# Another sequence of steps in the steady turns of a recurrent mixer

## What is computed

```python
mixed = hidden_states @ W_qkv.T
y = conv1d(mixed, conv_w)                  # causal, 4 taps, one filter per channel
q, k, v = split(silu(y))
z = hidden_states @ W_z.T
beta = sigmoid(hidden_states @ W_b.T)
g = -exp(A_log) * softplus(hidden_states @ W_a.T + dt_bias)
def step(S, (q_t, k_t, v_t, g_t, b_t)):    # a scan over the tokens
    S = S * exp(g_t)
    delta = (v_t - S.T @ k_t) * b_t
    S = S + outer(k_t, delta)
    return S, S.T @ q_t
h = o * silu(z)
h = h * rsqrt(mean(h * h) + EPS) * norm_weight
out = h @ W_out.T
```

## Time and profile before

| | us |
|---|---|
| median of 3 runs | 2748.21 (2746.57 to 2750.30) |
| the profiled execution | 2751.68 |
| its span | 2750.0 |
| busy: TensorE, VectorE, ScalarE, GpSimd | 2363.9, 1981.4, 1304.2, 839.3 |
| one steady turn, from 1104.50 to 1176.40 | 71.9 |

### The profile page before, as it was taken

The page is one execution under the profiler, slowest core; times in us unless marked ns, Lnnn a source line. Parts: engine busy times, 40 slices in busy tenths (PEclk is TensorE's granted clock), DMA queues, the critical chain, the costliest instruction groups (busy, mean ns, idle before and its releaser), DMA issues. The chain is left out here.

```text
span 2750.0 us, 53589 instructions
## 1 busy us (share of the span) xinstructions
PE 2363.9 (86%) x19286; PEld 1813.9 (66%) x19286; DVE 1981.4 (72%) x4757; ACT 1304.2 (47%) x3127; POOL 839.3 (31%) x698
## 2 busy tenths in 40 slices
PE   7999998997747998889899989878487958799998
PEld 6777776885725777777777777756374845577654
DVE  4898984333368898988888888897755436787772
ACT  0444443211256777767676777774130214455232
POOL 2111100000113333333333333334876037560110
PEclk9999998998568999999999999998778977899999
DMA  4221001001412221111122222233221862220000
GB/s 158 75 76 29 14 10 51 23 24 44 156 24 51 54 53 46 45 49 50 41 51 53 52 56 55 55 82 83 77 46 25 295 188 75 73 62 1 8 21 28
DMA packets 274614, 169.24 MB, mean 62 GB/s; under 512 B 182863, under 2 KB 250590, under 8 KB 274000
## 3 DMA queue, kind: packets, MB, share of 16 engines
q1 hardware_dynamic: 248221, 140.55, 18.0%
q0 software_dynamic: 26112, 25.03, 3.5%
HBM read 99.49 MB, written 73.45 MB: 63 GB/s over the span
## 5 line engine op out<-in xcount | busy, mean ns | idle before, releaser
L1405 POOL TENSOR_TENSOR qd<-decay,qm 114x456 f32<-114x456 f32 x128 | 162.0, 1285 | 551.8 <-DVE qm L1604 464.3
L2358 PEld LDWEIGHTS d_ps<-d_xT,resid 128*128 128x128 f32 x1024 | 198.0, 195 | 47.1 <-issue 29.7
L2358 PE MATMUL d_ps<-d_xT,resid 128*128 128x228 f32 x1024 | 216.5, 363 | 12.3 <-DMA d_xT<-normed_t 12.3
L1585 DVE TENSOR_TENSOR ue<-ue,elim_tmp 128x30 f32<-128x30 f32 (+14 forms) x480 | 210.2, 438 | 16.8
L3028 POOL DMA_INDIRECT s_eo<-rows_y,slots_all x128 | 153.2, 1197 | 147.4 <-POOLq L2795 109.4
L1583 DVE TENSOR_TENSOR elim_tmp<-ue 128x30 f32<-128x30 f32 (+14 forms) x480 | 178.6, 372 | 25.2 <-issue 9.8
L1647 DVE SCALAR_TENSOR_TENSOR y_v<-raw,taps,y_v 128x228 f32<-128x228 f32 x384 | 163.4, 498 | 45.0 <-ACT y_v L2025 45.0
L1987 ACT ACTIVATE decay<-d_ps,gates 114x114 f32<-114x114 f32 x512 | 137.9, 362 | 83.7 <-DVE nt L1617 48.6
L1647 DVE SCALAR_TENSOR_TENSOR y_qk<-raw,taps,y_qk 128x228 f32<-128x228 f32 x384 | 146.5, 455 | 23.3 <-ACT y_qk L2025 23.3
L1998 ACT ACTIVATE gl<-upto,gates 114x114 f32<-114x114 f32 x512 | 156.1, 392 | 0.5 <-PE d_ps L2346 0.2
L2334 PE MATMUL d_ps<-y_qk 64*114 64x228 f32 x512 | 73.8, 411 | 95.6 <-DVE nt L1617 57.0
(11 more groups left out here) (370 smaller groups left out, 5698.9 us busy)
## 6 DMA issues: line engine op xcount, KB each, us to landing
rows_x<-zero_row SPq DMA_DIRECT2D x4, 2048.0 KB
ue<-blocks_n SPq DMA_DIRECT2D x16, 512.0 KB, 5.1
blocks_u<-ue SPq DMA_DIRECT2D x16, 512.0 KB, 3.0
blocks_v<-on SPq DMA_DIRECT2D x16, 512.0 KB, 3.1
e_x<-rows_x SPq DMA_DIRECT2D x32, 256.0 KB, 4.5
e_gu<-L_ffn_w_gate_up SPq DMA_DIRECT2D x32, 256.0 KB, 4.6
rows_y<-e_y SPq DMA_DIRECT2D x32, 256.0 KB, 3.8
blocks_n<-nt SPq DMA_DIRECT2D x96, 64.0 KB
```

The costliest lines, as they stand in the source:

```text
L1405: pool.tensor_tensor(qd[p.par][s][:, hs(u), :].rearrange("p (a o b) t -> p a o b t", o=2, b=2)[:, :, o], e[o][:, :, :].rearrange("p (a b) ...
L1585: step = dve.tensor_tensor(ue[:, 0:j, j + 1:], ue[:, 0:j, j + 1:], part, ALU.subtract)
L2358: last = pe.matmul(ps[:, f % 2, (t % 2) * W:(t % 2 + 1) * W], w_qkv[:, k, t * 128:(t + 1) * 128], xT[:, k, :], start=(k == 0), stop=(k == ...
```

## The change

Nothing is added or removed: on GpSimd, VectorE, ScalarE and TensorE the same steps stand in another sequence. On VectorE the steps of the elimination lie closer together, gate_mean 1, gate_silu 0, query_mask 2 and weights 4 and 5 come after `turn_inverse`, and the convolution comes after weights 7. On TensorE the four `value` steps stand ahead of the four `join` steps, products 3 stands behind output_turn 1, and the row steps are regrouped. On GpSimd, query_decay 4 stands between gate_power 1 and gate_scale 1. On ScalarE the reads are regrouped to match. The diff, with its indent shortened by 16 columns:

```diff
@@ -1453,24 +1453,27 @@

 def iteration(p, a=True, proj=True, z=True, d=True):
     r, done, nxt = p.shift(-1), p.shift(-2), p.shift(1)
+    if z:
+        clear_x(r, 0)
     if a:
         query_decay(p, 0)
         query_decay(p, 1)
     if d:
         gate_power(done, 0)
         gate_scale(done, 0)
-    if z:
-        clear_x(r, 0)
     if a:
         query_decay(p, 2)
+    if z:
+        clear_x(r, 1)
+    if a:
         query_decay(p, 3)
     if d:
         gate_power(done, 1)
-        gate_scale(done, 1)
-    if z:
-        clear_x(r, 1)
     if a:
         query_decay(p, 4)
+    if d:
+        gate_scale(done, 1)
+    if a:
         query_decay(p, 5)
         query_decay(p, 6)
         query_decay(p, 7)
@@ -1663,57 +1666,52 @@
     r, done, nxt = p.shift(-1), p.shift(-2), p.shift(1)
     if z:
         eliminate(r, 1, 9)
-    if a:
-        query_mask(p, 0)
-    if z:
         eliminate(r, 9, 10)
-    if a:
-        weights(p, 0)
     if d:
         gate_mean(done, 0)
     if z:
         eliminate(r, 10, 14)
     if a:
+        query_mask(p, 0)
+        weights(p, 0)
         weights(p, 1)
-    if d:
-        gate_mean(done, 1)
     if z:
         eliminate(r, 14, 23)
     if a:
+        weights(p, 2)
+        weights(p, 3)
         query_mask(p, 1)
     if z:
         eliminate(r, 23, 24)
-        gate_silu(r, 0)
-    if a:
-        weights(p, 2)
-        weights(p, 3)
     if d:
         residual(done, 0)
     if z:
         eliminate(r, 24, 29)
-    if a:
-        weights(p, 4)
-        query_mask(p, 2)
-        weights(p, 5)
-    if z:
         eliminate(r, 29, 31)
         turn_inverse(r)
+    if d:
+        gate_mean(done, 1)
+    if z:
+        gate_silu(r, 0)
         gate_silu(r, 1)
     if a:
+        query_mask(p, 2)
+        weights(p, 4)
+        weights(p, 5)
         query_mask(p, 3)
-    if proj:
-        conv(nxt, 0, 1)
-        conv(nxt, 0, 2)
-        conv(nxt, 0, 3)
-    if d:
-        residual(done, 1)
-    if a:
         weights(p, 6)
         weights(p, 7)
     if z:
         gate_silu(r, 2)
+    if proj:
+        conv(nxt, 0, 1)
+    if d:
+        residual(done, 1)
+    if z:
         gate_silu(r, 3)
     if proj:
+        conv(nxt, 0, 2)
+        conv(nxt, 0, 3)
         conv(nxt, 1, 1)
         conv(nxt, 1, 2)
         conv(nxt, 1, 3)
@@ -1723,15 +1721,13 @@
         conv(nxt, 3, 1)
         conv(nxt, 3, 2)
         conv(nxt, 3, 3)
+        silu(nxt, 0)
     if z:
         gated(r, 0)
     if proj:
-        silu(nxt, 0)
+        silu(nxt, 1)
     if z:
         gated(r, 1)
-    if proj:
-        silu(nxt, 1)
-    if z:
         gated(r, 2)
         gated(r, 3)
     ch.end()
@@ -2080,97 +2076,98 @@

 def iteration(p, a=True, proj=True, z=True, d=True):
     r, done, nxt = p.shift(-1), p.shift(-2), p.shift(1)
+    if a:
+        decay_exp(p, 0)
     if d:
         gate_squares(done, 0)
-    if a:
-        decay_exp(p, 0)
-        decay_terms(p, 2)
-        decay_exp(p, 1)
-        decay_terms(p, 3)
+        gate_squares(done, 1)
     if proj:
         raw_read(nxt, 0)
         raw_read(nxt, 1)
+    if a:
+        decay_terms(p, 2)
+        decay_terms(p, 3)
+        decay_terms(p, 4)
+        decay_exp(p, 1)
+    if proj:
         raw_read(nxt, 2)
-    if d:
-        gate_squares(done, 1)
-    if proj:
         raw_read(nxt, 3)
-        raw_read(nxt, 4)
     if a:
         decay_exp(p, 2)
     if proj:
+        raw_read(nxt, 4)
         raw_read(nxt, 5)
+    if a:
+        decay_exp(p, 3)
+    if proj:
         raw_read(nxt, 6)
-    if a:
-        decay_terms(p, 4)
-        decay_exp(p, 3)
     if d:
         oT_read(done, 0)
+    if a:
+        decay_terms(p, 5)
+        decay_terms(p, 6)
     if z:
         gate_tanh(r, 0)
     if proj:
         raw_read(nxt, 7)
     if a:
-        decay_terms(p, 5)
         decay_exp(p, 4)
-        decay_terms(p, 6)
-        decay_terms(p, 7)
     if z:
         gate_tanh(r, 1)
     if a:
+        decay_terms(p, 7)
         decay_exp(p, 5)
-    if proj:
-        decay_terms(nxt, 0)
-        first_tap(nxt, 0)
+        decay_exp(p, 6)
     if z:
         gate_tanh(r, 2)
     if d:
         oT_read(done, 1)
+    if a:
+        decay_exp(p, 7)
+    if proj:
+        first_tap(nxt, 0)
+        decay_terms(nxt, 0)
+    if z:
+        gate_tanh(r, 3)
     if proj:
         first_tap(nxt, 1)
-    if a:
-        decay_exp(p, 6)
-        decay_exp(p, 7)
+        first_tap(nxt, 2)
     if z:
-        gate_tanh(r, 3)
         join_read(r, 0)
-        join_read(r, 1)
         rhs_read(r, 0, 0)
         rhs_read(r, 0, 1)
+        join_read(r, 1)
         join_read(r, 2)
-        rhs_read(r, 0, 2)
-        rhs_read(r, 0, 3)
+        join_read(r, 3)
         inverse_read(r, 0)
         inverse_read(r, 1)
-    if proj:
-        first_tap(nxt, 2)
-    if z:
         inverse_read(r, 2)
-        join_read(r, 3)
-        x_read(r, 0, 0)
-        x_read(r, 0, 1)
-        x_read(r, 0, 2)
-        inverse_read(r, 3)
+        rhs_read(r, 0, 2)
     if proj:
         first_tap(nxt, 3)
     if z:
+        x_read(r, 0, 0)
+        x_read(r, 0, 1)
+        inverse_read(r, 3)
+        rhs_read(r, 0, 3)
+        rhs_read(r, 1, 0)
+        x_read(r, 0, 2)
+    if proj:
+        decay_terms(nxt, 1)
+    if z:
         x_read(r, 0, 3)
-        rhs_read(r, 1, 0)
         rhs_read(r, 1, 1)
         rhs_read(r, 1, 2)
         x_read(r, 1, 0)
+        rhs_read(r, 1, 3)
     if proj:
         tanh(nxt, 0)
     if z:
         x_read(r, 1, 1)
-        rhs_read(r, 1, 3)
         x_read(r, 1, 2)
+        x_read(r, 1, 3)
     if proj:
         tanh(nxt, 1)
-    if z:
-        x_read(r, 1, 3)
-    if proj:
-        decay_terms(nxt, 1)

 def xT_read(g):
     act.wait_ge(r_t, g * 2 + 2)
@@ -2489,82 +2486,78 @@
 def iteration(p, a=True, proj=True, z=True, d=True):
     r, done, nxt = p.shift(-1), p.shift(-2), p.shift(1)
     if a:
+        products(p, 0)
         decay(p, 0)
-        products(p, 0)
         decay(p, 1)
     if proj:
         project(nxt, 0)
-    if a:
-        decay(p, 2)
-    if proj:
         project(nxt, 1)
         project(nxt, 2)
         project(nxt, 3)
-        project(nxt, 4)
     if a:
+        decay(p, 2)
         decay(p, 3)
     if proj:
+        project(nxt, 4)
         project(nxt, 5)
+        project(nxt, 6)
     if a:
         products(p, 1)
-    if proj:
-        project(nxt, 6)
     if d:
         output_turn(done, 0)
+        output_product(done, 0)
+    if a:
+        decay(p, 4)
+        decay(p, 5)
     if z:
         gate_product(r, 0, proj)
-    if a:
-        decay(p, 4)
     if proj:
         project(nxt, 7)
-    if d:
-        output_product(done, 0)
-    if a:
-        decay(p, 5)
-        products(p, 2)
     if z:
         gate_product(r, 1, proj)
     if a:
-        decay(p, 6)
+        products(p, 2)
     if z:
         gate_product(r, 2, proj)
     if a:
-        products(p, 3)
+        decay(p, 6)
+    if z:
+        gate_product(r, 3, proj)
+    if a:
+        decay(p, 7)
     if d:
         output_turn(done, 1)
     if a:
-        decay(p, 7)
-    if z:
-        gate_product(r, 3, proj)
+        products(p, 3)
     if d:
         output_product(done, 1)
     if z:
         value(r, 0, a)
+        value(r, 1, a)
+        value(r, 2, a)
+        value(r, 3, a)
         join(r, 0, a)
         join(r, 1, a)
-        value(r, 1, a)
         join(r, 2, a)
-        value(r, 2, a)
-        value(r, 3, a)
         join(r, 3, a)
         inverse(r, 0)
         inverse(r, 1)
+        inverse(r, 2)
+        inverse(r, 3)
         substitute(r, 0, 0)
-        inverse(r, 2)
         substitute(r, 0, 1)
         substitute(r, 0, 2)
-        inverse(r, 3)
         carry(r, 0)
         carry(r, 1)
         substitute(r, 0, 3)
+        substitute(r, 1, 0)
         carry(r, 2)
         carry(r, 3)
-        substitute(r, 1, 0)
         substitute(r, 1, 1)
+        substitute(r, 1, 2)
+        substitute(r, 1, 3)
         outputs(r, 0)
-        substitute(r, 1, 2)
         outputs(r, 1)
-        substitute(r, 1, 3)
         outputs(r, 2)
         outputs(r, 3)

```

## The result

The changed kernel takes 2791.64 us (median of 4 runs, 2787.53 to 2796.71), against 2748.98 for the kernel before in the same runs (2746.57 to 2750.30): a ratio of 1.0154, 95% interval 1.0135 to 1.0173, or 42.7 us more. The forecast was 2802, slower. The profiled execution took 2796.71 us, the longest of its four and 45.0 more than the one of before.

A forecast was written before the change was run, and what follows sets the result against it. Waits, not a full engine, bound a turn: elimination, chain to join 0, row steps, 71.8 us. New terms 33.8 + 1.4 + 13.7 + 26.9 = 75.8; 52 us over thirteen turns plus about 2 gives a 2802 median, range 2766 to 2840.

The forecast's parts named there:

- Stretch two: From turn_inverse's end to join 0's start: 7.84 us before, forecast to become 15.1 us (1.4 + 13.7).
- a chain through three engines: From gate_mean 1's end, work on GpSimd, TensorE and VectorE tied in a row, putting join 0 13.7 us later.
- Stretch one: The elimination, from its first instruction to turn_inverse's end: 37.40 us less 3.57 of moved steps, forecast 33.8 us.
- the sign of being right: For the elimination, a length of 33 to 35 us in the new timeline would confirm the forecast.
- the contention with GpSimd: GpSimd blocking VectorE in the elimination: 3 us freed, as much newly added, so 0; ends 2.5 better, 1.75 worse.
- TensorE's slack: TensorE has 28 us of work ahead of gate_product 2 against 33.8 us of elimination: some 6 us to spare.
- Rival (a): TensorE's hole ahead of gate_product 2 slows its clock: 2.0 us more a turn, 6.0 in all, 2828 us; chance 0.22.
- Stretch three: The row steps, from join 0 to the last gated: 26.54 us before, forecast 26.9, ends 25.4 to 28.5.
- Rival (b): Faster: VectorE's first-tap waits vanish if join 0 starts within about 11 us of turn_inverse; 2706 us; chance 0.11.
- Turn 1: The turn without `done` steps, where only products 3 behind two gate_products delays: about 2 us more.
- The range: Whole execution: good ends give 1.2 us a turn, 2766; rival (a) with the row steps' bad end gives 7.0, 2840.

The follow-up runs named there:

- e2: Changed kernel with gate_mean 1 put back into the elimination on VectorE, behind weights 1: 2776.74 us, ratio 1.0082 to the kernel before.
- e5: Changed kernel with two GpSimd steps exchanged, gate_scale 1 directly behind gate_power 1 and ahead of query_decay 4: 2801.8 us, ratio 1.0165 to the kernel before.
- e3: Changed kernel with both gate_mean 1 and gate_silu 0 put back into the elimination: 2780.84 us, ratio 1.0092 to the kernel before.
- x1: Kernel before with query_mask 2, weights 4 and 5 behind turn_inverse, convolution, products 3 and first taps moved; gate_mean 1, gate_silu 0 and GpSimd unchanged: 2722.0 us.
- x2: x1 with residual 1 moved ahead of conv 0 1 on VectorE: 2712.95 us, ratio 0.9854 to the kernel before.
- e4: Kernel before with VectorE's list alone in the changed order, other engines untouched: 2834.92 us, ratio 1.0301 to the kernel before.
- e6: e4 with three extra matmuls that nobody reads on TensorE ahead of gate_product 2: 2817.53 us, ratio 1.0227 to the kernel before.
- e7: Changed kernel with SyncE's two loads of the next inputs ahead of the last four stores of blocks: 2786.92 us, ratio 1.0117 to the kernel before.

## Why the prediction was right, and where its steps were off

**Stretch two: right, and the chain is the reason.** With M the end of gate_mean 1 (1160.47), the forecast was join 0 at M + 13.7; it came at 1174.17, M + 13.70. That the two agree to the hundredth is luck: gate_scale ends at M + 5.9 (forecast 6.1), and from there to join 0 it takes 7.8 (forecast 7.6). VectorE stands 5.14 (forecast 5), and value 3 waits 0.23 us for gate_silu 3, which the forecast had as just in time. The +7.74 instead of +7.3 is a matter of the starting point: the 7.84 of the earlier trace rows was one turn, the thirteen have 7.31 on average. But "a chain through three engines" was too narrow a picture. TensorE's own list and ScalarE's order end within a microsecond of GpSimd's, as e2 and e5 show; taking time out of one queue hands the wait to the next. With gate_mean 1 early again (e2) and gate_silu 0 as well (e3) the stretch is still 13.5 and 12.0, and what holds it up in e3 is query_decay 4 ahead of gate_scale 1, which the forecast counted as 1.05 us of GpSimd's time and not as a wait for query_mask 2. Only x1 and x2, where those two are early and gate_scale 1 does not stand behind query_decay 4, come near the 7.3 of before.

**Stretch one: mis-sized by 1.2 us.** The forecast was 33.8, and the sign of being right 33 to 35; 32.64 was measured. The work moved is as forecast; the contention with GpSimd, which I took as 0, is a gain. VectorE's groups by line show it as a mean over turns 903 to 1810 (count, busy us, mean ns, idle before), before first, then after:

```profile
L1585 DVE TENSOR_TENSOR ue<-ue,elim_tmp 128x30 f32<-128x30 f32 (+14 forms) x390 | 176.4, 452 | 13.7
L1583 DVE TENSOR_TENSOR elim_tmp<-ue 128x30 f32<-128x30 f32 (+14 forms) x390 | 145.8, 374 | 20.1 <-issue 9.8
```

```profile
L1588 DVE TENSOR_TENSOR ue<-ue,elim_tmp 128x30 f32<-128x30 f32 (+4 forms) x360 | 154.9, 430 | 12.4
L1586 DVE TENSOR_TENSOR elim_tmp<-ue 128x30 f32<-128x30 f32 (+4 forms) x360 | 128.9, 358 | 20.1 <-issue 9.8
```

The same thirty pairs of a turn take 22 and 16 ns less each: 30 x 0.038 = 1.1 us. In the turn shown the four L1588 rows at 1139.61, 1143.89, 1151.42 and 1153.35 take 1.15, 1.98, 1.10 and 1.09 us where instructions of the same size beside them take 0.41, 0.40, 0.35 and 0.33: 3.83 us of blocks. The same reckoning gives about 5.0 for the turn of before, 1.75 of it at 1145.95. Of these 3.46 left the elimination, where 3 was forecast: gate_scale 1's 1.75, 1.34 at query_decay 4 and 5, and 0.37 beside clear_x 0. But what came anew is 2.33 and not as much again: gate_scale 0 does block (1.58 of the 1.98), the query_decays cost one block of 0.75 more, and the clear_x at its new place nothing. That half of the term was mis-sized. e2 and x1 fit this: gate_mean back in the elimination cost 0.6 instead of 1.35, and x1's elimination fell by 3.1 with 1.62 of steps moved. The Trainium skill ("SBUF — State Buffer", the section on SBUF's two separate sides) says that VectorE and GpSimd share one port pair as an exclusive lock and that the loser waits for the winner's whole instruction. The trace agrees for gate_scale: the instruction at 1143.89 ends at 1145.87, and gate_scale 0 beside it at 1143.62 + 2.00 = 1145.62. It does not agree for gate_power, which reads and writes 114x16: gate_power 0 runs beside the elimination from 1140.47 to 1143.55, and the six instructions of the elimination that lie within that time take 0.41 us each, as elsewhere.

**TensorE's slack: wrong, and it cost nothing here.** I reckoned 28 us of work ahead of gate_product 2 and some 6 us of slack. The hole ahead of decay 3 came as forecast (2.50, from 1138.23's row), but behind it the two decays ran in 1.84 us instead of 0.93 (granted clock 0.50 from 1138.20 to 1140.10), and TensorE waited 0.94 us for an oT and 0.63 for a raw_read. It was done with products 2 only at about 1160.3, and waited 0.83 us ahead of gate_product 2. Over twelve turns this wait is 0.7 us a turn on average and at most 1.5, so that is all the slack there was. The step that failed is the subtraction: a difference of busy times leaves out holes and the slow clock behind them.

**Rival (a): the mechanism is real, its condition did not hold.** The hole of 2 to 4 us that it wanted ahead of gate_product 2 was 0.83, since TensorE came late, the gate_product ran in 1.97, and the granted clock from 1159 to 1174, where stretch two lies, is 1.00. That "the early hole may take the slow stretch instead, where it is hidden" is what happened in the turn shown (1138.23). e4 has the condition (3.55), and e6 takes the price out of stretch two, 1.5 us a turn where I had put 2.0, though in its profiled execution 1.2 of them come back in stretch one.

**Stretch three: right in size, in part by luck.** 27.17 against 26.9. The thirteen turns lie between 26.07 (the one shown) and 28.52. In them TensorE stands 1.7 us a turn, with no releaser in the trace; before has no such stops in this stretch, and the forecast has no term for them. The two turns with the fewest of them (0.38 us) take 26.07, less than forecast. e7, where SyncE's DMAs come in another order, takes 0.46 off the mean.

**Rival (b)** needed join 0 within 11 us of `turn_inverse`. x1 and x2 meet that (8.87 and 7.80) and are faster, by 33 and 41 us, and in x2 VectorE's waits for first taps fall from 39.1 to 1.0 us (turns from 903 to 1810); (b)'s 2706 was the right size for a version of the change, not for this one.

**The sum**: the turn rose by 3.38 us, 44 in thirteen, where 4.0 to 4.1 was forecast, 52 to 53. Stretch one is 13 x 1.0 = 13 us better than forecast, stretch two 13 x 0.48 = 6.2 worse, stretch three 13 x 0.15 = 2.0 better. Turn 1, for which 2 us was forecast, grew by 0.24. The range was not added up from its own terms: all the good ends together (2.5, 0.5 and 1.5) give 0.5 us a turn less than before and not 1.2 more, and (a) with the bad end of stretch three gives 7.6 and not 7.0.

## What to carry to other kernels

A step moved behind a milestone is costed by what is tied behind it in every queue, not by its own length: 1.35 us of gate_mean stood at the head of 13.7 us until join 0, and a query_mask of 0.54 held up gate_scale through a query_decay in front of it. Move the steps that nothing on the way to the next milestone waits for, and leave those that head a chain where they are. Where several queues end together, shortening one gains nothing; look for the version in which the chain's head starts earlier.

## What the runs showed of the hardware

GpSimd's affine_select over 128x1024, in the middle of VectorE's undivided convolution, took 10.70 us in after (row at 1180.11), while in this turn of before it took 1.27:

```profile
1174.88 1.27 POOL L1447 TENSOR_SCALAR_AFFINE_SELECT ue<-ue 128x1024 f32<-128x1024 f32 x1 [7.87 <-DMA ue<-blocks_n]
```

It ended at 1190.81. VectorE's convolution lies beside it without a gap and ends at 1180.79 + 8.88 = 1189.67 (its row is the last in VectorE's fence above). In twelve of the thirteen turns it took 9.8 to 12.2 us and ended 1.1 us behind the convolution. In the other (from 1104.37) it took 6.57 and ended within the convolution, whose last 24 instructions then took 10.87 us instead of 8.88. By all appearance a run of VectorE instructions that follow each other closely mostly keeps GpSimd out for as long as it lasts; that was not tested apart. In the turn shown it cost nothing, since the next elimination starts only at 1202.70, some 10 us later. And a wait can cost more than its length: TensorE's 3.5 us in e4 took another 1.5 us behind it, by the clock (1.97 us of work in 3.52, at a granted clock of 0.71).
